# Second layer's routed experts: hidden rows computed turned, with a ring of three weight buffers filled tile by tile

## The reference, cut to what matters

```
routed = for each expert e: mask(ids == e) * ((silu(xs @ wg[e][:, :512]) * (xs @ wg[e][:, 512:])) @ wd[e])
shared = (silu(x @ sg[:, :512]) * (x @ sg[:, 512:])) @ sd
x = x + attention(xn) + routed + shared        # 8 experts, top 1; wg: 256 x 1024, wd: 512 x 256, all float32
```

## Time and profile before

| | us |
|---|---|
| median of three timed runs | 1352.87 |
| their lowest and highest | 1349.44, 1354.07 |
| the profiled execution, its device time | 1343.85 |
| the profiled execution, its span | 1342.1 |
| first matmul of `experts1`, from the span's start | 1117.84 |
| first routed matmul, first matmul behind the routed loop's last output | 1161.81, 1300.19 |

### The profile page before, as it was taken

How to read it: one execution, slowest core, us unless ns; L and a number is a source line. 1 busy time by engine, 2 the same in 40 slices (tenths; PEclk the granted TensorE clock), 3 DMA queues, 4 the chain that set the end, 5 groups by cost and what they waited for, 6 DMA issues and landing times. The chain is left out here.

```text
span 1342.1 us, 20324 instructions
## 1 busy us (share of the span) xinstructions
PE 1266.8 (94%) x7210; PEld 1026.4 (76%) x7245; DVE 686.2 (51%) x1374; ACT 520.2 (39%) x1123; POOL 681.7 (51%) x535
## 2 busy tenths in 40 slices
PE   6589999999879998999999999999999998999998
PEld 5468888888658887888788888888888884666655
DVE  6996555555866578665654335434343342222223
ACT  4345566666465333334233343333433322011110
POOL 3536877775503465666765656556565550000013
PEclk9589999999999998999999999999999998999999
DMA  9603888885405220222121112211111107511213
GB/s 321 195 1 88 180 182 191 178 175 107 165 1 168 67 68 25 66 72 64 61 66 56 52 36 67 63 52 51 36 52 48 36 14 280 184 48 44 64 47 114
DMA packets 99204, 126.99 MB, mean 95 GB/s; under 512 B 11713, under 2 KB 84033, under 8 KB 98977
## 3 DMA queue, kind: packets, MB, share of 16 engines
q1 hardware_dynamic: 84176, 99.59, 23.5%
q0 software_dynamic: 14928, 26.10, 9.9%
HBM read 97.70 MB, written 27.95 MB: 94 GB/s over the span
## 5 line engine op out<-in xcount | busy, mean ns | idle before, releaser
L1528 PE MATMUL a_p_p<-a_xr,a_wr 128*128 128x512 f32 x1152 | 308.6, 403 | 2.4 <-DVE g_x L2078 2.4
L1528 PEld LDWEIGHTS a_p_p<-a_xr,a_wr 128*128 128x128 f32 x1152 | 206.6, 189 | 42.5 <-DVE g_x L2078 3.1
L1846 POOL TENSOR_TENSOR a_sqsum<-a_sqsum,a_sq 128x512 f32<-128x512 f32 x60 | 77.8, 1296 | 232.5 <-ACT a_sq L1731 232.5
L1814 POOL TENSOR_TENSOR a_wr<-g_hold,a_wr 128x768 fp32r<-128x768 f32 x63 | 122.3, 1941 | 20.1 <-DVE a_wr L1878 20.1
L1914 DVE SCALAR_TENSOR_TENSOR a_gated<-a_th,a_p_o 128x512 f32<-128x512 f32 x64 | 44.0, 688 | 159.0 <-ACT a_sq L1731 159.0
L409 POOL DMA_INDIRECT acc<-l_ye,g_slot_token x64 | 102.1, 1595 | 33.6 <-issue 14.7
L1848 POOL TENSOR_TENSOR a_gr<-a_gated,a_gr 128x512 fp32r<-128x512 f32 x64 | 97.7, 1527 | 23.8 <-DVE a_gr L1918 23.8
L1541 PE MATMUL a_p_p<-a_wvr,a_xr 128*128 128x512 f32 x384 | 108.9, 421 | 0.6 <-DVE a_xr L1872 0.6
L1155 POOL DMA_DIRECT2D out<-e_ye x23 | 12.5, 544 | 178.7 <-DVE e_ye L1304 178.7
L1599 PE MATMUL a_p_w<-a_gr,l_wo_r 128*128 128x512 f32 x384 | 100.9, 398 | 2.3 <-POOL a_gr L1848 2.3
L1583 PE MATMUL a_p_o<-a_sc,a_v 128*128 128x128 f32 x512 | 89.8, 278 | 6.7 <-DVE a_sc L1894 6.7
(11 more groups left out here) (273 smaller groups left out, 2735.6 us busy)
## 6 DMA issues: line engine op xcount, KB each, us to landing
g_hold<-in_Wqkg SPq DMA_DIRECT2D x64, 384.0 KB, 3.2
g_hold<-in_gate_up SPq DMA_DIRECT2D x64, 192.0 KB
g_hold<-in_Wv SPq DMA_DIRECT2D x16, 512.0 KB, 4.8
e_up<-in_gate_up SPq DMA_DIRECT2D x8, 1024.0 KB, 14.1
l_down<-in_down SPq DMA_DIRECT2D x64, 96.0 KB
acc<-l_zero SPq DMA_DIRECT2D x2, 2176.0 KB, 11.7
l_lists<-acc SPq DMA_DIRECT2D x8, 512.0 KB, 4.9
e_down<-in_down SPq DMA_DIRECT2D x8, 512.0 KB, 12.2
```

The source lines that it names most:

```text
L1528: mm = pe.matmul(dst[:, :], wr[n % 2][:, wp, kk, c * P:(c + 1) * P], xr[n // H1 % 2][:, xp, kk, :], start=(kk, xp, wp) == (0, 0, 0), stop= ...
L1814: pool.tensor_tensor(wr[n % 2][:, 1, :, :], w[n % 2], wr[n % 2][:, 0, :, :], ALU.subtract).then_inc(w_parts, 1)
L1846: pool.tensor_tensor(sqsum[b % 2][:, :], sqsum[b % 2][:, :], sq[a % 2][:, :], ALU.add).then_inc(summed, 1)
```

## The change

The routed hidden rows are computed turned: TensorE now holds a 128 x 128 block of `up` and streams the 128 tokens of `xT` past it, eight times per half where there were two matmuls of 512 columns. `p_g` and `p_u` then have hidden values on the partitions, and VectorE's product is `hT` itself. The transposes of `h`, ScalarE's copy, `p_h` and `h` go away.

The matmuls no longer choose the expert by a register; it is chosen when the weights are loaded. SP reads the tile's expert number and fills one of three buffers of `up` and `down` with it, once for each of the 23 tiles. A buffer is filled again once the matmuls of the tile three before it are done.

```
-        up = m.sb("up", [P, E1, KD, 2 * F1])
-        down = m.sb("down", [P, E1, HC, D])
+        WR = 3
+        up = [m.sb(f"up{s}", [P, KD, 2 * F1]) for s in range(WR)]
+        down = [m.sb(f"down{s}", [P, HC, D]) for s in range(WR)]
...
+            def weights(t):
+                e = sp.value_load(g["tile_expert"][0:1, t:t + 1], min_val=0, max_val=E1 - 1)
+                if t >= WR:
+                    sp.wait_ge(u_done, U["r", t - WR, 0] + 1)
+                sp.dma_start(up[t % WR][:, :, :], io["gate_up1"][bass.ds(e, 1), :, :].rearrange("a (k p) n -> p (a k) n", p=P))\
+                    .then_inc(up_in[t % WR], 16)
+                if t >= WR:
+                    sp.wait_ge(y_done, Y["r", t - WR, 0] + 1)
+                sp.dma_start(down[t % WR][:, :, :], io["down1"][bass.ds(e, 1), :, :].rearrange("a (k p) n -> p (a k) n", p=P))\
+                    .then_inc(down_in[t % WR], 16)
...
-            for e in range(E1):
-                sp.dma_start(up[:, e, :, :], up_v[e, :, :, :]).then_inc(weights_in, 16)
-                sp.dma_start(down[:, e, :, :], down_v[e, :, :, :]).then_inc(weights_in, 16)
+            for t in range(WR):
+                weights(t)
+            tokens(2)
+            tokens(3)
             for t in range(3, RT1):
                 rows(t)
-            tokens(2)
-            tokens(3)
+                weights(t)
...
                 if half == 0:
-                    expert[t] = pe.value_load(g["tile_expert"][0:1, t:t + 1], min_val=0, max_val=E1 - 1)
+                    pe.wait_ge(up_in[t % WR], 16 * (t // WR + 1))
                     pe.wait_ge(xT_ready, t + 1)
                 pe.wait_ge(free, u - 1)
-                for k in range(KD):
-                    mm = pe.matmul(bank[u % 2][:, :], xT[t % 2][:, k, :],
-                                   up[:, bass.ds(expert[t], 1), k, half * F1:(half + 1) * F1].rearrange("p a n -> p (a n)"),
-                                   start=k == 0, stop=k == KD - 1)
+                for c in range(HC):
+                    at = half * F1 + c * P
+                    for k in range(KD):
+                        mm = pe.matmul(bank[u % 2][:, c * P:(c + 1) * P],
+                                       up[t % WR][:, k, at:at + P], xT[t % 2][:, k, :], start=k == 0, stop=k == KD - 1)
...
             def output(t):
                 y = Y["r", t, 0]
-                pe.wait_ge(hT_ready, t + 1)
+                pe.wait_ge(h_ready, U["r", t, 0] + 1)
+                pe.wait_ge(down_in[t % WR], 16 * (t // WR + 1))
...
-            pe.wait_ge(weights_in, 32 * E1)
             for t in range(RT1 + 1):
                 if t < RT1:
                     hidden(t, 0)
-                if t >= 1:
-                    turn_hidden(t - 1)
-                if t < RT1:
                     hidden(t, 1)
```

More of the change, by code:

```diff
@@ L1083, in experts1 @@
         gate = [m.sb(f"gate{s}", [P, F1]) for s in range(2)]
-        h = [m.sb(f"h{s}", [P, F1]) for s in range(2)]
         hT = [m.sb(f"hT{s}", [P, HC, P]) for s in range(2)]
@@ L1091, in experts1 @@
         p_u = [m.ps(f"p_u{s}", [P, F1]) for s in range(2)]
-        p_h = m.ps("p_h", [P, HC, P])
         p_y = [m.ps(f"p_y{s}", [P, 512]) for s in range(2)]
-        (weights_in, x_in_psum, xT_ready, g_done, u_done, gate_ready, h_ready, h_in_psum, hT_ready, y_done, y_kept,
+        (x_in_psum, xT_ready, g_done, u_done, gate_ready, h_ready, y_done, y_kept,
          routed_added, y_stored) = (m.sem(n) for n in (
-            "weights_in", "x_in_psum", "xT_ready", "g_done", "u_done", "gate_ready", "h_ready", "h_in_psum",
-            "hT_ready", "y_done", "y_kept", "routed_added", "y_stored"))
+            "x_in_psum", "xT_ready", "g_done", "u_done", "gate_ready", "h_ready", "y_done", "y_kept", "routed_added", "y_stored"))
         routed_in = [m.sem(f"routed_in{s}") for s in range(BATCH)]
@@ L1100, in experts1 @@
         xe_in = [m.sem(f"xe_in{s}") for s in range(3)]
+        up_in = [m.sem(f"up_in{s}") for s in range(WR)]
+        down_in = [m.sem(f"down_in{s}") for s in range(WR)]
         ye_stored = [m.sem(f"ye_stored{s}") for s in range(2)]
@@ L1118, in _ @@
         def _(sp):
-            up_v = io["gate_up1"].rearrange("e (k p) n -> e p k n", p=P)
-            down_v = io["down1"].rearrange("e (k p) n -> e p k n", p=P)
+            def weights(t):
[8 more added lines that the diff above has]
+                    .then_inc(down_in[t % WR], 16)
             def tokens(group):
@@ L1163, in _ @@
         def _(pe):
-            expert = {}
             def shared_unit(group, f):
@@ L1200, in hidden @@
                 if half == 0:
-                    expert[t] = pe.value_load(g["tile_expert"][0:1, t:t + 1], min_val=0, max_val=E1 - 1)
+                    pe.wait_ge(up_in[t % WR], 16 * (t // WR + 1))
                     pe.wait_ge(xT_ready, t + 1)
                 pe.wait_ge(free, u - 1)
-                for k in range(KD):
-                    mm = pe.matmul(bank[u % 2][:, :], xT[t % 2][:, k, :],
-                                   up[:, bass.ds(expert[t], 1), k, half * F1:(half + 1) * F1].rearrange("p a n -> p (a n)"),
-                                   start=k == 0, stop=k == KD - 1)
-                mm.then_inc(done, 1)
-            def turn_hidden(t):
-                pe.wait_ge(h_ready, U["r", t, 0] + 1)
-                if t >= 1:
[L1213 to L1216, removed]
+                for c in range(HC):
[3 more added lines that the diff above has]
+                                       up[t % WR][:, k, at:at + P], xT[t % 2][:, k, :], start=k == 0, stop=k == KD - 1)
+                mm.then_inc(done, 1)
             def output(t):
                 y = Y["r", t, 0]
-                pe.wait_ge(hT_ready, t + 1)
+                pe.wait_ge(h_ready, U["r", t, 0] + 1)
+                pe.wait_ge(down_in[t % WR], 16 * (t // WR + 1))
                 pe.wait_ge(y_kept, y - 1)
                 for c in range(HC):
-                    mm = pe.matmul(p_y[y % 2][:, 0:D], hT[t % 2][:, c, :],
-                                   down[:, bass.ds(expert[t], 1), c, :].rearrange("p a n -> p (a n)"), start=c == 0, stop=c == HC - 1)
+                    mm = pe.matmul(p_y[y % 2][:, 0:D], hT[t % 2][:, c, :], down[t % WR][:, c, :], start=c == 0, stop=c == HC - 1)
                 mm.then_inc(y_done, 1)
@@ L1262, in silu @@
                 act.activation(gate[u % 2][:, :], p_g[u % 2][:, :], ACT.Silu).then_inc(gate_ready, 1)
[L1264 to L1268, removed]
             for what, t, f in units:
                 silu(U[what, t, f])
[L1272 to L1275, removed]
         @block.vector
@@ L1294, in times @@
                     if t >= 2:
-                        dve.wait_ge(h_in_psum, t - 1)
-                    dst = h[t % 2][:, :]
+                        dve.wait_ge(y_done, Y["r", t - 2, 0] + 1)
+                    dst = hT[t % 2][:, :, :].rearrange("p c n -> p (c n)")
                 dve.tensor_tensor(dst, gate[u % 2][:, :], p_u[u % 2][:, :], ALU.mult).then_inc(h_ready, 1)
```

## The result

The changed kernel's median is 1342.3 us over four runs (1339.56 to 1343.38), where the kernel before has 1353.15: a ratio of 0.9922 with a 95% interval from 0.9897 to 0.9947. The forecast was 1344.9 us, 8.0 us less.

The account below looks back on a forecast made before the run. TensorE's own work in the routed loop was taken as the bound. Per tile 0.43 us removed less 0.08 added gives 0.35, 8.0 us over 23 tiles: 1352.87 - 8.0 = 1344.9 us, range 1339 to 1353.

Parts of the forecast that it names:

- What bounds the kernel: Routed loop: TensorE's own work end to end, 5.82 us per tile, so what leaves TensorE leaves the time.
- The term removed: Routed tiles: transposes of h go, 0.43 us each on TensorE, 9.9 us over 23; ScalarE's copy and register load worth nothing.
- The term added: Routed halves on TensorE: thirty-two 128-column records at 0.110 us take 3.52 us instead of 3.44, giving back 0.08 per tile.
- the 5.43 to 5.50 that was to show the forecast: Routed loop, sign in the changed profile: iterations of 5.43 to 5.50 us.
- the straight line through 512 and 256 columns: TensorE's pace: a line through records of 0.4295 and 0.216 us gives 0.109 us at 128 columns.
- The ring: Routed loop's weight buffers: transfers take 4.89 us of a 5.47 us tile, 89%, so nothing was put on transfers.
- the same sum: Routed loop's transfers per tile: weight bytes at 386 GB/s, 4.07 us, plus 0.81 us for other traffic.
- The round: Refilling up in the loop: SP's work, transfers and landing in a row take 9.7 us, less than two tiles' 10.9.
- The slow rival: Routed loop: the ring starves TensorE, 6.4 us slower at 292 GB/s; 12% for a costly ring, a third of it slower.
- The window from 1105 to 1110 us: Trace before the routed loop: a queue just started showed 292 GB/s, at which a tile takes 6.19 us.
- The weight-load rival: Routed halves: TensorE bound by weight loads over 32 records, at 0.190 us each 51 us slower, 1404; 7%.
- The ratio of 2.5: Routed halves: by the skill page four small matmuls cost 2.5 times one large, making the kernel some 107 us slower; not taken.

Follow-up runs that it names:

- e1_resident: The changed kernel without its ring: all eight experts' weights brought in once, tile t using fixed expert t modulo 8; 1335.59 us, 0.9939 to the kernel before.
- e2_ring_only: The kernel before with the ring of three buffers alone, keeping 512-column matmuls and transposes; 1344.08 against 1343.51 us, ratio 0.9997.
- e5_64cols: e1_resident with each matmul of the routed hidden rows streaming 64 of 128 tokens, weight loads as many; 1342.6 us, 0.9975 to the kernel before.
- e6_down_twice: The changed kernel with each tile's down loaded a second time into an unread buffer; 1350.76 us, 1.0036 to the kernel before.
- after: The changed kernel as first measured and profiled, against the kernel before; median 1342.3 us, ratio 0.9922.
- e3_again: The changed kernel measured once more, nothing altered, against the kernel before; 1336.53 against 1343.51 us, ratio 0.9942.
- e9_changed: The changed kernel measured once more on another chip, against the kernel before; 1337.19 against 1345.53 us, ratio 0.9938.

## Why the prediction was right

**What bounds the kernel.** TensorE's own work did. With the hidden rows turned a tile takes 5.52 us with the ring and without (e1_resident), and unturned 5.82 with the ring and without (e2_ring_only).

**The term removed.** 0.43 us of transposes per tile went entirely, and ScalarE's copy and the register loads were worth nothing, as forecast; e2_ring_only has no register load on TensorE and the tile of before, and for the copy nothing is left, since 0.43 less the 0.13 of the next term is the whole 0.30.

**The term added.** It was taken at 0.110 us a record, between 0.109 and 0.111. It measured 0.1115, so that 0.13 us per tile are given back where 0.08 was taken, and the gain is 7.0 us where 8.0 was forecast. That is outside the 7.3 to 8.7 that the terms allowed, and the tile of 5.52 us is outside the 5.43 to 5.50 that was to show the forecast. The better row was the one from the attention stage, at 0.111; the straight line through 512 and 256 columns left out the weight load, which at 128 columns takes about as long as the columns (e5_64cols).

**The ring.** It starved nothing, as forecast. Demand stayed under the rate, and the same sum gave the 6.24 us of e6_down_twice. The round was put at 9.7 us at most; it was 9.2 us in the median and 10.0 at most, so that bound was a little low, and 1.0 us of the two tiles was left. Its parts came out otherwise: SP's was 1.7 us from the issue of `down` to that of `up`, where up to 2.7 was allowed for the whole, and landing took 7.0 to 8.2 us where transfers and landing together were put at 7.0. The slow rival would have come with one buffer less. The window from 1105 to 1110 us that spoke for it, 292 GB/s, held a short burst at the end of the attention stage; the loop, whose queues are fed all the time, moved 331 GB/s and e6_down_twice 378.

**The weight-load rival** was closer than its price looked. Records with a 190 ns load follow each other at 0.11 us, so 0.190 is no pace; but the load is what seems to bound, at about 0.11. The Trainium skill's page "TensorE: Matmul & The Clock Gate" gives in its section "LDWEIGHTS (loading the stationary operand)" the columns of the held block divided by 1.2 GHz, which is 107 ns for 128. The 0.108 and 0.112 us a record of e5_64cols agree with it as a pace, though the trace records one such load with 190 ns. The ratio of 2.5 that the same page's section on issue gaps would give did not show.

**The median.** The first comparison showed 10.9 us less, the two later ones 7.0 and 8.3, and the loop accounts for 7.0. The intervals of the later two hold 0.9948; that of the first ends at 0.9947. So it is partly luck that the first median, 1342.3, came within 2.6 us of the forecast: some 4 us of its 10.9 are not from the change as far as the runs show. Whether there is a real difference of 1 us or so outside the loop is open; no stage length shows one. The starts of the stage lie between 1115.8 and 1124.0 us in these profiles, without order by kernel, and that is as large as the change itself. Much of this wander goes with the clock: of the 45 timed executions of the kernel before that stood beside the experiments, the eight with a mean granted clock of 0.970 or less took 1346.6 to 1350.3 us and the eight with 0.977 took 1341.2 to 1344.7.

## What to carry to other kernels

Choosing what TensorE holds so that the result comes out with the right axis on the partitions removes transposes at a small price, here 0.13 us for the 0.43 that went, with 128 columns streamed past a held block of 128. At 64 columns streamed each record still cost 0.110 us, so fewer columns saved nothing there. A ring of buffers needs two sums, the bytes per tile by the rate of full queues and the length of one round by the tiles between a buffer's release and its next use; here the second one decided between two buffers (48 us slower) and three (free, with 1.0 us left at worst). To size a change of some microseconds in a kernel whose earlier stages wander by as much, compare the length of the stage that was changed.

## What the hardware showed that was not expected

In e5_64cols the loop's second iteration lost the clock. The window from 1165 to 1185 us has it granted at 0.74, and the chain shows the second iteration at half pace:

```profile
1165.38 1.73 PE e_p_g L1205 x16
...
1170.08 3.46 PE e_p_g L1205 x16
1173.54 3.41 PE e_p_u L1205 x16
...
1180.76 1.73 PE e_p_g L1205 x16
```

From 1170.08 to 1180.76 TensorE was at its lower level, 1.2 GHz, and the iteration took 10.68 us where the later ones take 5.47: 5.2 us lost. The later tiles are 0.05 us shorter than those of e1_resident, 1.1 us in all, and the stage is 4.3 us longer (221.1 and 216.8): so this loss is why the kernel with less to stream was slower. It came right behind the wait of 1.0 us in the second iteration, before which TensorE had been busy at the full clock. after, e1_resident, e3_again and e9_changed have the same wait in the same place, and their clock stayed at 1.00 across it. Why it fell in this one was not tried, and only one execution was profiled.
